# Where the convolution of a Mamba scan stands in its pipeline turn, and when GpSimd makes the decay products

## What is computed

```python
proj = u @ W_in.T
z, x, B_toks, C_toks, dt_toks = jnp.split(proj, ...)        # 256, 256, 64, 64, 4 columns
xBC = conv(concat([x, B_toks, C_toks]), conv_w, taps=4, causal, per channel) + conv_b
x, B_toks, C_toks = split(silu(xBC))
dt = softplus(dt_toks + dt_bias);  dA = exp(dt * -exp(A_log))
for t in tokens:                                             # 4 heads of 64, state 64
    S = S * dA[t] + dt[t] * outer(x[t], B[t])
    y[t] = S @ C[t]
y = (y + D_param * x) * silu(z)
out = y @ W_out.T
...
x = x + mamba(layernorm(x)) + experts0(layernorm(x))
x = x + attention(layernorm(x)) + experts1(layernorm(x))
```

## Time and profile before

| What | Value |
|---|---|
| Median of 3 runs | 1523.24 us (1514.99 to 1524.38) |
| Profiled execution | 1502.72 us, its span 1501.2 us |
| Mean granted TensorE clock | 0.98 of full speed |
| TensorE matmuls busy | 1392.2 us (93% of the span) |
| VectorE busy | 828.9 us (55%) |
| ScalarE busy | 512.8 us (34%) |
| GpSimd busy | 657.1 us (44%) |

### The profile page before, as it was taken

How to read it: one execution, slowest core, us unless ns; L and a number is a source line. 1 busy time by engine, 2 the same in 40 slices (tenths; PEclk the granted TensorE clock), 3 DMA queues, 4 the chain that set the end, 5 groups by cost and what they waited for, 6 DMA issues and landing times.

```text
span 1501.2 us, 29754 instructions
## 1 busy us (share of the span) xinstructions
PE 1392.2 (93%) x10881; PEld 1133.1 (75%) x10881; DVE 828.9 (55%) x2307; ACT 512.8 (34%) x1102; POOL 657.1 (44%) x814
## 2 busy tenths in 40 slices
PE   7999999999999999899998899999999988888886
PEld 6888889999999999666665566666666557777775
DVE  4556434444444444588888677777777623322256
ACT  2212122222222222333332455555545443333331
POOL 2355423333333332554443245445444455666561
PEclk9999999999999999999999999999999999999998
DMA  5894921111111111500000110111100012222357
GB/s 183 145 116 66 93 62 50 47 47 50 50 50 47 47 50 36 172 1 0 0 0 22 44 43 23 44 36 30 44 23 16 2 30 73 86 85 85 108 187 234
DMA packets 69936, 94.89 MB, mean 63 GB/s; under 512 B 13401, under 2 KB 57433, under 8 KB 69808
## 3 DMA queue, kind: packets, MB, share of 16 engines
q1 hardware_dynamic: 51152, 53.92, 16.3%
q0 software_dynamic: 18656, 39.23, 8.4%
HBM read 60.66 MB, written 32.44 MB: 62 GB/s over the span
## 4 chain that ended last, share of the span: by engine, by line
PE 78%; DVE 9%; issue 6%; another core or an unknown queue 3%; POOL 2%; ACT 1%; DMA 0%; DVEq 0%; POOLq 0%; ACTq 0%
PE score L1657 47%; PE mixed L1657 18%; PE side L1657 8%; PE side L1873 2%; DVE ARENA L1406 2%; DVE WGU L1499 2%; PE side L1667 1%; POOL ARENA L731 1%; PE mixed L2047 1%; DVE stats L1061 1%; PE side L2040 1%; DVE X L1614 1%; DVE X L1524 1%; DVE ARENA L1390 0%
## 5 line engine op out<-in xcount | busy, mean ns | idle before, releaser
L757 POOL DMA_INDIRECT XN<-xn_rows,slot_tok x111 | 108.6, 978 | 233.0 <-PE side L1873 205.5
L1657 PE MATMUL score<-xT,HT 128*128 128x128 f32 x1136 | 208.0, 275 | 0.0
L764 POOL DMA_INDIRECT y_rows<-sh_gu,slot_row x149 | 146.3, 982 | 125.6 <-ACT sh_gu L941 89.8
L792 POOL TENSOR_SCALAR_AFFINE_SELECT ARENA<-ARENA 128x256 f32<-128x256 f32 x256 | 104.5, 432 | 193.7 <-ACT ARENA L973 193.1
L1499 DVE TENSOR_REDUCE WGU<-score 128x2 f32<-128x256 f32 (+1 forms) x256 | 130.8, 553 | 104.8 <-PE score L1657 101.9
L1657 PEld LDWEIGHTS score<-xT,HT 128*128 128x128 f32 x1136 | 166.8, 192 | 0.0
L1288 DVE TENSOR_TENSOR HT<-sh_gu,score 128x128 f32<-128x128 f32 (+1 forms) x149 | 71.2, 478 | 146.7 <-issue 74.6
L973 ACT ACTIVATE ARENA<-score 128x768 f32<-128x768 f32 x128 | 103.8, 811 | 137.4 <-PE score L1657 137.0
L699 POOL DMA_INDIRECT lists<-token_no,w_in x128 | 125.1, 977 | 40.0 <-issue 28.5
L1657 PE MATMUL score<-ARENA 32*128 32x256 f32 (+1 forms) x2048 | 127.4, 355 | 14.1 <-DVE WGU L1499 8.1
L1263 DVE COPY xT<-WGU 128x256 f32 x142 | 45.6, 362 | 169.8 <-PE score L1657 169.0
(11 more groups left out here) (251 smaller groups left out, 2651.2 us busy)
## 6 DMA issues: line engine op xcount, KB each, us to landing
WGU<-in_gu SPq DMA_DIRECT2D x8, 1024.0 KB
WGU<-y_rows SPq DMA_DIRECT2D x32, 256.0 KB, 3.1
ARENA<-y_rows SPq DMA_DIRECT2D x32, 256.0 KB
xn_rows<-XN SPq DMA_DIRECT2D x24, 256.0 KB
X<-in_u SPq DMA_DIRECT2D x16, 256.0 KB
ARENA<-in_dn SPq DMA_DIRECT2D x8, 512.0 KB
out<-X SPq DMA_DIRECT2D x16, 256.0 KB
y_rows<-sh_gu,slot_row POOLq DMA_INDIRECT x149
```

The costliest lines, as they stand in the source:

```text
L757: x["got"][j % ring].mark(eng.indirect_dma_start(XG[j % ring], None, xn_rows[l], bass.IndirectOffsetOnAxis(slot_tok[:, j:j + 1], 0)))
L764: x["out"][j % RING].mark(eng.indirect_dma_start(y_rows[g], bass.IndirectOffsetOnAxis(slot_row[:, j:j + 1], 0), YO[j % RING], None))
L792: ins = eng.affine_select(out=m, in_=m, compare_op=ALU.is_ge, fill=0.0, base=0, pattern=[[0, 2], [1, P]], channel_multiplier=-1)
L1657: return eng.matmul(o, l, r, start=start, stop=stop)
```

## The change

TensorE projects B and C (part 4) at the start of the turn, ahead of `decay_sums`, and x (parts 2 and 3) where it projected all of them before; `M["proj"]` is marked after x. The wait for the taps of the sequence before moves with the first of them. VectorE does the taps of a sequence in the turn in which it is projected (`conv_taps(new)`, behind `scan_parts`), no more in the turn after; `conv_silu(conv)` stands directly behind `gate_y`. ScalarE puts `conv_tanh` ahead of `decays` and `conv_first` ahead of the state and z. GpSimd waits for the end of `conv_silu` ahead of CE, then makes piece 0, then waits for WM and makes pieces 1 and 2. The first turns are written out apart.

```diff
--- before.py
+++ after.py
@@ -726,6 +726,8 @@
 
             if pieces[0] == 0:
                 M["dec"].wait(eng, r.n, 1)
+            elif pieces[0] == 1:
+                M["wm"].wait(eng, r.n, 1)
             for a in pieces:
                 av = DT3[:, a, bass.ds(r.n * CH, CH), :].rearrange("p c h -> p (c h)")
                 ins = eng.tensor_tensor(
@@ -741,14 +743,14 @@
             M["ce"].mark(eng.tensor_tensor(CE, CE, CT[r.u][:, P:SEQ].unsqueeze(1).broadcast_to([P, MH // 2, P]), ALU.mult))
 
         def mamba(new, r):
-            ahead = new and not (isinstance(new.n, int) and new.n == 0)
+            ahead = new and r
             if ahead:
-                decay_factors(new, range(PIECES - 1))
+                M["xs"].wait(eng, new.n)
             if r:
                 carry_factors(r)
             if ahead:
-                M["xs"].wait(eng, new.n)
-                decay_factors(new, range(PIECES - 1, PIECES))
+                decay_factors(new, range(1))
+                decay_factors(new, range(1, PIECES))
 
         def gather_tile(l, j):
 
@@ -911,16 +913,19 @@
             M["zt"].mark(act(ZT.rearrange("p k t -> p (k t)"), bank[1][:, :], ACT.Tanh, scale=0.5))
 
         def mamba(new, conv, r, old):
-            if r:
+            starting = r and conv and isinstance(r.n, int) and r.n == 0
+            if starting:
                 decays(r)
             if conv:
                 conv_tanh(conv)
+            if r and not starting:
+                decays(r)
+            if new:
+                conv_first(new)
             if r:
                 state_copy(r)
             if r:
                 z_tanh(r)
-            if new:
-                conv_first(new)
         def experts(l):
             x = EX[l]
 
@@ -1451,13 +1456,13 @@
             if old:
                 gate_y(old)
             if conv:
-                conv_taps(conv)
-            if r:
-                scan_parts(r)
-            if conv:
                 conv_silu(conv)
             if old:
                 add_y(old)
+            if r:
+                scan_parts(r)
+            if new:
+                conv_taps(new)
             if r:
                 z_silu(r)
         for t, stages in enumerate(tile_turns(NJ)):
@@ -1847,15 +1852,23 @@
                 carried(c)
 
         def mamba(new, conv, r, old):
-            if r:
+            at = new.n if new and isinstance(new.n, int) else None
+            if new and at != 0:
+                if at == 2:
+                    turn_parts(r)
+                M["cv"].wait(eng, new.n, 1)
+                project(new, (4,))
+            if at == 1:
+                M["proj"].mark(project(new, (2, 3)))
+                decay_sums(of(0))
+            if r and at != 2:
                 decay_sums(r)
             if old:
                 project_y(old)
-            if r:
+            if r and at != 2:
                 turn_parts(r)
-            if new and not (isinstance(new.n, int) and new.n == 0):
-                M["cv"].wait(eng, new.n, 1)
-                M["proj"].mark(project(new, (2, 3, 4)))
+            if new and at != 0 and at != 1:
+                M["proj"].mark(project(new, (2, 3)))
             if r:
                 state(r)
                 if not (isinstance(r.n, int) and r.n == 0):
```

## The result

The changed kernel takes 1541.19 us (median of 14 runs, 1529.51 to 1552.3), the kernel before, on the same chips, 1517.82 (14 runs, 1507.58 to 1529.59). The ratio is 1.0151, 95% interval 1.0121 to 1.0180: 22.9 us slower, between 18.4 and 27.3. A second series on another chip gave 1494.97 against 1479.83, ratio 1.0114 (1.0089 to 1.0139), 16.9 us slower. The profiled execution of the changed kernel took 1542.88 us, its span is 1541.2.

A forecast was written before the change was run, and what follows sets the result against it. It took the kernel to be bound by a ring of projection, state, z, scan, gate and taps, 12.65 us a turn. Edges and turns, 4.8 + 9.8 + 1.5 = 16.1 us, gave 1539.3 us, range 1522 to 1550.

The forecast's parts named there:

- the new ring: Steady turns: B and C, `decay_sums` to `turn_parts`, x, first tap and taps in series, 13.47 us against 12.65; +9.8 over 12.
- the wait for the taps: TensorE at the head of each steady turn: waits 1.4 us for the taps where it waited 0.65.
- Everything else in the turn fits beside the ring: Steady turns: the other work of VectorE, ScalarE and GpSimd fits beside the 13.47 us and costs nothing.
- GpSimd's part: GpSimd's products moved outside VectorE's two-operand work: gain nothing, as the conflict was 1.3 us of VectorE time, with slack.
- the tail: Behind turn 15: end of its projection to `decay_sums(15)` takes 17.5 us instead of 16.0, +1.5.
- The head: Turns 2 and 3: piece 0 holds XW, B and C of turn 3 start at 637.4, their x ends 4.8 us late.
- the clock falls: Rival: TensorE's idling lowers its clock to 0.94, 0.5 us more a turn, +6, total 1545; chance 0.08.

The follow-up runs named there:

- the run with the old projection: Changed kernel with x, B and C projected together behind `turn_parts`, as before the change; ratio 1.0113 to the kernel before.
- the filled wait: Changed kernel with three unused matmuls added ahead of TensorE's wait for the taps; ratio 1.0167 to the kernel before, 1.0118 the second time.
- the first round of taps early: Kernel before with ScalarE's first tap ahead of `z_tanh` and VectorE's first three tap operations ahead of `z_silu`; ratio 1.0030.
- B and C early: Changed kernel with B and C marked by their own event and tapped ahead of `scan_parts`, `add_y` behind it; ratio 1.0052 to the kernel before.
- late GpSimd stream: Changed kernel with all three of GpSimd's decay pieces behind WM; 1563.3 us in one run.

## Why the prediction came out as it did

Predicted were 1539.3 us and +16.1; measured were 1541.19, and +22.9 (18.4 to 27.3) in one series, +16.9 (13.2 to 20.6) in the other. The direction, the new ring and its place were right. That 1539.3 lies 1.9 from 1541.19 is partly luck: the median of the kernel before came out 5.4 lower (1517.82) than the 1523.24 that I added to, and the difference was 6.8 larger than my sum.

- **The new ring** was summed as 13.47 and is 13.40; the wait for the taps as 1.4 and is 1.34, in 12 waits of 15.9 in all. The order is the predicted one: first tap 0.04 behind x, taps 0.03 behind the first tap, a microsecond behind WM. The rows of before held to a hundredth, and what was over is `decay_sums` to `turn_parts` in one piece: B and C start to x start is 5.86, where I had 5.93. Term: +9.0 instead of +9.8. That the wait grew by 0.70 a turn and the turn by 0.75 says the same: no work was added, only waiting.
- **Everything else in the turn fits beside the ring**: right. `add_y` waits for TensorE, 18.0 in 12, GpSimd's two waits have nobody behind them. That there is a second ring of nearly the same length, through z, gate and `project_y`, I did not see; the run with the old projection showed it (13.52).
- **GpSimd's part gains nothing**: right in the steady turns, shown by undoing it (13.40 in both). At the tail I had priced it as a loss only, and undone it held the gate's product (1.87 instead of 0.69), so that TensorE waited 1.5 us longer for it: there the part gains.
- **The head** was +4.8 and is 0.33 less: 10.62 instead of 10.95. That GpSimd's piece blocks XW to 0.27 behind its end came out to the hundredth (641.36 and 641.63); the handovers around it were 0.3 shorter in sum than I had them.
- **The tail** was 17.5 and is 17.35.
- These three make 14.8 us. The stage grew by 20.0. The rest is the term that was missing, and the step that failed is the rival *the clock falls*: "With 10% idle I expect 1.00", with a chance of 0.08. The window reads 0.98. The turns at 646.58 and 715.60 are 2.0 and 1.6 longer than 13.40, and the one at 811.04 took 7.55 to its x instead of 5.86, 1.7 more: 5.3 in all. I had priced the case at +6, as 0.94 and 0.5 us in every turn; it came as 1.6 to 2.0 us in three turns, with 0.98 in the mean. So the chance was wrong, and that the price was near is luck.
- From the 20.0 of the stage (18.3 against the second profile of before) to the ratios, 22.9 and 16.9, I have no cause to name: both intervals hold the 20.0, the first only just misses the 18.3, and unchanged code differs by more.

**Left open.** Why the clock falls in those turns, and why in the same three in each of three executions. Idle time has a part in it, as the filled wait shows. It isn't its amount alone: with the old place of the projection TensorE idled 1.5 us in each of the 12 turns from 664.27 to 826.47, for the gate, and was granted 1.00 there, while the projection of turn 2 of the same profile took 4.51 behind a wait of 0.84. Whether it is the place of the gap within the turn was not tried.

## What to carry to other kernels

Before a step is moved into the turn of its producer, write down the ring that it closes: everything that the in-order engines have queued between the wait and the mark counts, on each engine, also what has nothing to do with the step. A step that is a turn behind its producer is off that ring. In the steady turns it paid to move a few of its instructions into a gap (1.17 us here; 12.23 a turn instead of 12.65) and not the whole (13.40), but no version here was faster in the total beyond its interval. So price the first and last turns apart; in two of the versions (the first round of taps early, and B and C early) they took back what the steady turns gave.

## What the runs showed of the hardware

- **The rows behind a short gap can run at the lower clock.** With 1.34 us of idling ahead of each turn, they did in 2 of 12 steady turns (4 to 15) in each of five profiles (three of the changed kernel, and the ones with the old and with the late GpSimd stream). With 0.64 they never did, in two profiles, and with the gap filled neither. At the edge shorter gaps did: the 12 rows of turn 2's projection took 4.5 instead of 2.86 behind a wait of 0.83 or 0.84 in four profiles, one of them of the kernel before, and 2.86 behind the same wait in others.
- **GpSimd is held up as well.** I wrote that no row of before shows VectorE holding up GpSimd. In the run with the old GpSimd stream it does: two pieces that started 0.02 behind the last operation of `conv_silu` took 4.28 instead of 3.75, CE, started behind XW, 0.91 instead of 0.73, and one piece, started behind WM, 2.87 instead of 1.89. The Trainium skill ("SBUF — State Buffer", Who interferes with whom) says that issue order decides who blocks; these rows agree with it, and at the head, where piece 0 had started 0.08 ahead of XW, so does the 2.09 of XW.
- **Unchanged code scatters.** The stages ahead of the first projection took 606.21 and 631.94 us in two executions of the same kernel, and a turn of the ring 12.65 in both. A difference of a few us is read from the stage, and its effect on the total only from many runs.
